# Left-overs of x ahead of the biases, row maxima sent from ScalarE's queue, ones around the first turn, Hadamard products two steps later

## The reference, cut to what matters

```python
x = x + attn_a(layernorm(x))   # 16 heads of 16: softmax(Q K^T / 4) V Wo^T, with biases
x = x + ffn(layernorm(x))      # fwht(silu(x W1^T) * (x W3^T)) W2^T, 1024 hidden
x = x + attn_b(layernorm(x))   # gated running memory, decay 0.95
x = x + ffn(layernorm(x))      # the same weights again
```

## Time and profile before

| | |
|---|---|
| runs | 582.75, 585.02, 587.06 us |
| profiled execution | 586.45 us, of which the span from first to last instruction is 584.7 us |
| TensorE busy | 564.5 us (97% of the span), 3274 instructions |
| VectorE busy | 380.5 us (65%) |
| ScalarE busy | 304.8 us (52%) |
| GpSimd busy | 179.1 us (31%) |
| mean granted clock of TensorE | 0.991 |
| chain that ended last | PE 82%, ACT 5%, POOL 4%, DVE 3%, SPq 2% |

### The profile page before, as it was taken

How to read it: one execution, slowest core, us unless ns; L and a number is a source line. 1 busy time by engine, 2 the same in 40 slices (tenths; PEclk the granted TensorE clock), 3 DMA queues, 4 the chain that set the end, 5 groups by cost and what they waited for, 6 DMA issues and landing times.

```text
span 584.7 us, 8896 instructions
## 1 busy us (share of the span) xinstructions
PE 564.5 (97%) x3274; PEld 389.8 (67%) x3274; DVE 380.5 (65%) x730; ACT 304.8 (52%) x559; POOL 179.1 (31%) x207
## 2 busy tenths in 40 slices
PE   7999999999999987999999999999999999999997
PEld 4553343344335433368988888898777888888887
DVE  6787898888888896745453544558887436344333
ACT  2657878867886886752334232344445233424221
POOL 4351456552545397820101010014333010101000
PEclk9988999999999999999999999999999999999999
DMA  5246530330034130020000000000000010010101
GB/s 153 63 124 231 158 118 2 111 109 3 20 113 132 55 127 3 3 72 2 1 0 1 1 1 2 1 0 1 1 1 1 0 37 1 0 37 2 36 1 37
DMA packets 17995, 25.74 MB, mean 44 GB/s; under 512 B 3048, under 2 KB 11240, under 8 KB 17568
## 3 DMA queue, kind: packets, MB, share of 16 engines
q1 hardware_dynamic: 16768, 24.11, 12.6%
q10 hardware_dynamic: 1184, 1.05, 0.6%
HBM read 10.89 MB, written 5.24 MB: 28 GB/s over the span
## 4 chain that ended last, share of the span: by engine, by line
PE 82%; ACT 5%; POOL 4%; DVE 3%; SPq 2%; issue 2%; DMA 1%; DVEq 0%; POOLq 0%; ACTq 0%
PE PS L369 79%; PE PS L380 2%; POOL xTl L1253 1%; ACT xf L774 1%; DVE PR L1222 1%; ACT PR L890 1%; ACT qf L788 1%; ACT xTh L774 1%; DVE XNs L1007 1%; ACT PR L953 1%; DMA ring<-mT 1%; POOL xf L1301 1%; DVE mxr L1026 1%; POOL XNs L1302 1%; SPq L258 1%
## 5 line engine op out<-in xcount | busy, mean ns | idle before, releaser
L369 PE MATMUL PS<-xTh,ring 128*128 128x512 f32 x608 | 188.7, 392 | 0.0
L1026 DVE TENSOR_REDUCE mxr<-PS 128x1 f32<-128x512 f32 x256 | 163.1, 681 | 30.7 <-PE PS L369 30.1
L890 ACT ACTIVATE PR<-PS 128x512 f32<-128x512 f32 x256 | 138.5, 602 | 41.6 <-PE PS L369 41.5
L369 PEld LDWEIGHTS PS<-xTh,ring 128*128 128x128 f32 x608 | 113.2, 188 | 23.6 <-issue 1.7
L369 PE MATMUL PS<-xTl,ring 128*128 128x512 f32 x304 | 110.3, 391 | 0.4 <-POOL xTl L1253 0.4
L369 PE MATMUL PS<-ring 48*128 48x512 f32 (+1 forms) x512 | 101.3, 456 | 6.2 <-DVE mxr L1026 4.4
L1171 DVE TENSOR_TENSOR PR<-PR,PS 128x512 f32<-128x512 f32 x64 | 43.8, 684 | 90.7 <-PE PS L369 71.0
L369 PEld LDWEIGHTS PS<-ring 50*128 50x128 f32 (+1 forms) x512 | 42.1, 187 | 85.1 <-ACT PR L890 57.2
L774 ACT ACTIVATE AOh<-PR 128x512 fp32r<-128x512 f32 x72 | 45.5, 632 | 101.8 <-DVE PR L1171 89.8
L1253 POOL TENSOR_TENSOR xTl<-xf,xTh 128x512 fp32r<-128x512 f32 x30 | 43.3, 1457 | 138.3 <-ACT xTh L774 138.3
L1018 DVE TENSOR_TENSOR AOl<-PR,AOh 128x512 fp32r<-128x512 f32 x72 | 51.1, 710 | 50.3 <-ACT AOh L774 50.3
(11 more groups left out here) (135 smaller groups left out, 629.8 us busy)
## 6 DMA issues: line engine op xcount, KB each, us to landing
ring<-qh SPq DMA_DIRECT2D x48, 128.0 KB, 2.7
ring<-ql SPq DMA_DIRECT2D x24, 128.0 KB, 2.7
ring<-weight_scratch SPq DMA_DIRECT2D x3, 1024.0 KB, 4.9
weight_scratch<-in_w SPq DMA_DIRECT2D x2, 1024.0 KB, 6.7
X<-in_x SPq DMA_DIRECT2D x3, 512.0 KB, 6.6
out<-X SPq DMA_DIRECT2D x6, 256.0 KB, 2.2
ring<-AOh SPq DMA_DIRECT2D x8, 128.0 KB, 2.7
ring<-AOl SPq DMA_DIRECT2D x4, 128.0 KB, 2.7
```

What stands on the lines that cost most here:

```text
L369: return nc.tensor.matmul(dst, lhsT, rhs, start=start, stop=stop, skip_group_check=True)
L890: nc.scalar.activation(PR[:, j % 8, :], PS[:, kq_bank(j), :], ACT.Exp, scale=HD ** -0.5)\
L1026: nc.vector.tensor_reduce(mxr[:, S % 2, blk, TT * p + t:TT * p + t + 1], PS[:, QK0 + i % 3, :], AX.X, ALU.max, negate=True).then_inc(max_d ...
```

## The change

Six edits.

- **VectorE, start:** the left-overs of x (`xTl`) are taken before the wait for the bias DMAs and `sbm`. Of the four statistics of sequence 1, two move behind `stack_rows(0)` and `(1)`.
- **TensorE, start:** stacks 0 and 1 first do the four products with `xTh` each, then the two with `xTl` each. TensorE waits for both halves of `x_hi` ahead of the first. In the other projections the order is the same as before. ScalarE does `stack_hi(1)` before it rounds the second weight matrix.
- **First maxima rows:** the pair of DMAs for `mrow_in` of the first group is issued by ScalarE, directly behind the copy into `mT`, and not by SyncE.
- **Ones:** at U = 10 and U = 12 of the lead, TensorE does one `keep_busy` of 384 columns.
- **Hadamard products:** `HAD_AT` goes from (14, 16, 26, 28) to (16, 17, 26, 28); ScalarE's copies and GpSimd's left-overs of the first two go with them (GpSimd's to steps 17 and 18, where the second stands behind the division of step 18). `output_lo(6)` goes from step 6 to step 13.
- **Weights:** the four left-overs of W3 (`W_LIN`) are taken by VectorE, each behind its own cast at steps 23 to 26, and GpSimd keeps the four of W1.

```diff
-HAD_AT = (14, 16, 26, 28)
+HAD_AT = (16, 17, 26, 28)
...
+            pe.wait_ge(x_hi, 2)
+            for i in range(2):
+                pe.wait_ge(swlo_done, i + 1)
+                project_stack(i, False)
+            pe.wait_ge(x_lo, 2)
+            for i in range(2):
+                project_stack(i, True)
...
+                else:
+                    keep_busy(1, PS[:, 0, :], FILL)
...
-            pe.wait_ge(llo_done, 8)
+            pe.wait_ge(llo_done, 4)
+            pe.wait_ge(lin_done, 4)
...
+            stack_hi(1)
             weights_hi(1)
-            stack_hi(1)
...
             max_evacuate(0, OB)
+            act.wait_ge(mt_ready, 1)
+            for blk in range(2):
+                act.dma_start(*max_copy(0, blk)).then_inc(mrow_in, DMA)
...
+            for dt in range(KD):
+                dve.wait_ge(x_hi, dt + 1)
+                lo(xTl[:, 0, dt, :], PS[:, dt, :], xTh[:, 0, dt, :]).then_inc(x_lo, 1)
             dve.wait_ge(mask_done, 1)
             dve.wait_ge(sbias_in, 8 * DMA)
...
-            for t in range(TT):
+            for t in range(2):
+                tile_statistics(TT + t, TT + t)
+            stack_rows(0)
+            stack_rows(1)
+            for t in range(2, TT):
                 last = tile_statistics(TT + t, TT + t)
...
                 nc.vector.tensor_copy(h, raw.bitcast(F32)).then_inc(lhi_done, 1)
+                if w == W_LIN:
+                    dve.wait_ge(lhi_done, 4 * w + i + 1)
+                    lo(raw, raw.bitcast(F32), h).then_inc(lin_done, 1)
...
-                if s == 6 and b:
+                if s == (13 if b == BATCH - 1 else 6) and b:
                     output_lo(2 * b)
...
-                if b == BATCH - 1 and SPLIT_AT <= s < SPLIT_AT + 8:
+                if b == BATCH - 1 and SPLIT_AT <= s < SPLIT_AT + 4:
```

More of the change, by code:

```diff
@@ L164, in build @@
         w_in = [sem(f"w_in{g}") for g in range(3)]
-        lhi_done, llo_done, mem_hi, mem_lo = (sem(n) for n in ("lhi_done", "llo_done", "mem_hi", "mem_lo"))
+        lhi_done, llo_done, lin_done, mem_hi, mem_lo = (
+            sem(n) for n in ("lhi_done", "llo_done", "lin_done", "mem_hi", "mem_lo"))
         g_ready, u_ready, sg_done, hf_done, hh_done, hl_done, y_ready = (
@@ L240, in rest_rows, with max_copy @@
                     for r in zip(*(rows(qk, part, blk) for blk in range(2))) for blk, r in enumerate(r)]
+        def max_copy(S, blk):
+            b, g = S // GROUPS, S % GROUPS
+            r = HALF * blk + MROW
+            return ring[r:r + 2, b % 2, QI, 2 * g:2 * g + 2, :].bitcast(F32), mT[16 * blk:16 * blk + 16, :]
         block = ctx.enter_context(nc.Block())
@@ L274, in _, with ring_load @@
                                  AOf[0:2, :].unsqueeze(1).broadcast_to([2, PAIRS - p, SEQ])).then_inc(ones_in, DMA)
-            def ring_load(b, n, parts_=range(2)):
-                for part in parts_:
+            def ring_load(b, n):
+                for part in range(2):
                     sp.wait_ge((qk_hi, qk_lo)[part], 4 * b + n + 1)
@@ L282, in max_rows @@
             def max_rows(S):
-                b, g = S // GROUPS, S % GROUPS
                 sp.wait_ge(mt_ready, S + 1)
                 for blk in range(2):
-                    r = HALF * blk + MROW
-                    sp.dma_start(ring[r:r + 2, b % 2, QI, 2 * g:2 * g + 2, :].bitcast(F32),
-                                 mT[16 * blk:16 * blk + 16, :]).then_inc(mrow_in, DMA)
+                    sp.dma_start(*max_copy(S, blk)).then_inc(mrow_in, DMA)
             def weights_in(w):
@@ L307, in _ @@
             ring_load(0, 2)
-            ring_load(0, 3, (0,))
-            max_rows(0)
-            ring_load(0, 3, (1,))
+            ring_load(0, 3)
             for e in range(2):
@@ L399, in project_qk, with project_rows, project_stack, project_rest @@
                     last.then_inc(qk_ready, 1)
-            def project_rows(weights, bank, first):
-                ops = [(1, 1, 0), (0, 1, 0), (1, 1, 1), (0, 1, 1), (0, 0, 0), (0, 0, 1)]
+            def project_rows(weights, bank, left):
+                ops = [(0, 0, 0), (0, 0, 1)] if left else [(1, 1, 0), (0, 1, 0), (1, 1, 1), (0, 1, 1)]
                 for i, (lo, r, kt) in enumerate(ops):
[L405 to L409, removed]
+                    last = mm(PS[:, bank, :], weights(lo, kt), xt(0, kt)[r], i == 0 and not left, i == 1 and left)
                 return last
-            def project_stack(i):
+            def project_stack(i, left):
                 p, w = i // 2, i % 2
-                project_rows(lambda lo, kt: stack_weights(lo, w)[:, kt, p * P:(p + 1) * P], STACK_BANK[i], i == 0)\
-                    .then_inc(stk_ready, 1)
+                last = project_rows(lambda lo, kt: stack_weights(lo, w)[:, kt, p * P:(p + 1) * P], STACK_BANK[i], left)
+                if left:
+                    last.then_inc(stk_ready, 1)
+            def project_rest(left):
+                last = project_rows(lambda lo, kt: rest_weights(lo)[:, kt, :], REST_BANK, left)
+                if left:
+                    last.then_inc(qk_ready, 2)
             def project_v(b, half, part, bank=MB):
@@ L508, in _ @@
             pe.wait_ge(pad_done, 1)
[L509 to L512, removed]
+            pe.wait_ge(x_hi, 2)
[5 more added lines that the diff above has]
+                project_stack(i, True)
             pe.wait_ge(rwlo_done, 1)
-            project_rows(lambda lo, kt: rest_weights(lo)[:, kt, :], REST_BANK, False).then_inc(qk_ready, 2)
+            for left in (False, True):
+                project_rest(left)
             def beside_maxima(U):
                 if U < 2:
-                    project_stack(2 + U)
+                    for left in (False, True):
+                        project_stack(2 + U, left)
                 elif U < 6:
@@ L1056, in _ @@
                                     ALU.mult).then_inc(sbm_done, 1)
-            for dt in range(KD):
-                dve.wait_ge(x_hi, dt + 1)
-                lo(xTl[:, 0, dt, :], PS[:, dt, :], xTh[:, 0, dt, :]).then_inc(x_lo, 1)
             def stack_rows(i):
```

4 lines of the change are left out of this document (1 added, 3 removed).

## The result

| | before | after |
|---|---|---|
| median of ten runs | 587.07 us (582.75 to 588.72) | 582.76 us (581.49 to 583.29) |
| profiled execution | 586.45, span 584.7 | 581.49, span 579.7 |
| mean granted clock of TensorE in it | 0.991 | 1.00 |

What follows compares the result with a forecast made beforehand. TensorE, busy nearly all the time, was taken as the bound, so gains come only where it waits or runs slowly. 586.45 - 3.05 - 0.15 - 3.3 - 1.6 + 2.7 = 581.0 us, range 578.5 to 584.4.

Steps and rivals of the forecast that it cites:

- Start, 3.05: Start: TensorE's wait for x's left-overs goes, first score at 15.3, 22 maxima from 21.0; 3.05 us gained, low clock included.
- Turn, 0.15: Turn: maxima's rows land earlier from ScalarE, ones fit beside the maxima's pace, TensorE arrives at 37.95; 0.15 us gained.
- Clock behind the turn, 3.3: Behind the turn: with the 1.03 us idle filled, clock stays at 1.00, steps 1 to 5 take 5.44; 3.3 us gained.
- First two products, 1.6: Last batch: the 2.61 us wait before the first Hadamard product goes, 0.5 before the second is new; net 1.6 us gained.
- Last two products, 2.7 lost: Last batch: left-overs on VectorE delay the third and fourth Hadamard products; 2.7 us lost, bound below 1.1.
- Rival 3: Last batch: new waits in steps 26 and 28 lower the clock, 3.4 us at half speed costing 1.7: 582.7; chance 0.12.
- Or the clock falls anywhere: Sign for the whole kernel: the prediction is wrong if TensorE's clock falls at any place; no size given.
- Rival 1: Behind the turn: the clock still falls, so the 3.3 us is not gained: 584.3; chance 0.17.
- rival 2: Last batch: VectorE has room for its left-overs, so the loss is only 1.1: 579.4; chance 0.14.
- Rival 4: Last batch: VectorE's left-overs held up like the worst casts, 1.15 each, 4.6 more: 585.6, slower than before; chance 0.07.

Runs made afterwards that it cites:

- late left-overs: Kernel after with VectorE's four left-overs of W3 moved behind its last reading of a Hadamard product: 579.40 us, ratio 0.987.
- the best of all: Kernel after with W3's left-overs behind VectorE's last Hadamard reading and ScalarE's two maxima-row DMAs behind its second copy of values: 578.92 us, ratio 0.9897.

## Why the prediction was right

- **What bounds the kernel.** Right: what was won and lost came from waits of TensorE, from the order of its start or from its clock, in the three places named, and arrived at the end (5.01 us at the fourth product, 5.0 in the span).
- **The sum.** 5.4 foretold, 5.0 measured in the profiles. In part this is luck: three gains were priced 0.06, 0.39 and 0.46 too high and the loss 0.55 too high, and more than half of the error cancels.
- **Start, 3.05.** Right to 0.06, and the marks with it (first score 15.37 for 15.3, the row of maxima 21.11 for 21.0). I put the gain down to the left-overs of x; the run with them moved back shows that the order of the stacks carries it in a good execution. The sum included the low clock behind the old wait, and rightly for the execution that I read: the run with the weights edit alone, where it did not fall, has its row of maxima at 22.71, so that 1.4 of the 2.99 are the clock and 1.6 the new order. In an execution like that one the start gains only 1.6.
- **Turn, 0.15.** Mis-sized: -0.24. I took 1.3 us for ScalarE's two DMAs from SyncE's row of 1.38; they took 1.92. The sentence "the transpose that waits for it then starts about where it does today" failed by that: the copy of values came at 32.84 and TensorE waited 0.63 for it.
- **Clock behind the turn, 3.3.** The mechanism is right and shown: with the ones 1.00, without them 0.50 for ten microseconds. The size is 2.84, since steps 1 to 5 took 5.95 (42.60 less 36.65) and not 5.44: the eight scores of steps 1 and 2 took 1.83, where eight take 1.33 later on, and I had taken the second batch's pace for theirs. Of these 0.5 us a wait of 0.15 for ScalarE, at 38.06, has a row; the rest stays open. What keeps the clock is the ones, not the earlier rows of maxima (without the ones it fell in eleven of twelve runs, with SyncE's rows and the ones it was 0.999 or 1.00 in five of six); for the rows the prediction named a gain in time of 1.6 us that nobody was waiting for once the start was earlier and the ones were in place.
- **First two products, 1.6.** Right in the execution profiled (1.57, with the wait of 0.51 for the 0.5 foretold).
- **Last two products, 2.7 lost.** Right in sign, in place and in who waits for whom; the size is 2.15. The waits are 0.57 and 1.48, where I had 0.9 and 1.6. Counted from the output projection of step 18, the add came 1.63 late (11.47 against 9.84) where I had 1.9. The first two left-overs took 2.35 and not 1.5, and a cast at 227.93 took 1.40 beside GpSimd's second product's left-over; against that, GpSimd was through at 235.54, so that the sixth cast took 0.41 and only one left-over of VectorE stood beside its three. The last two took 0.69 and 0.98.
- **Rival 3** was underrated with 0.12: by the mean clock something like it happened in half of the runs, and the median, 582.76, is its 582.7 and not the forecast's 581.0. "Or the clock falls anywhere" was moreover among the signs named for being wrong. "Against: the 2.61 before the first product did not" was read from one execution. That wait lowered the clock in four of the five profiles that have it (the start, the turn and the weights edit alone, and the late left-overs with the old Hadamard steps; not in before) and, by the mean clock, in eleven of twelve runs of the last of these. That the lower half of the clocks of the kernel after belongs to the new waits is inferred: from the second window without the ones, and from the twelve runs of the two kernels that lack these waits, none of which was below 0.999. The kernel before moved too, from the median of three, 585.02, to 587.07 of ten. Both moved up, and so the difference stayed near the forecast, which is luck: 5.4 foretold, 4.3 on the medians, 3.8 by the ratio.
- **Rivals 1, 2 and 4** did not happen. Rival 1 does as soon as the ones are taken out; rival 2's time of 579.4 is reached, by another way than its own, when the left-overs are placed behind the readings. Rival 4's price of 1.15 a left-over was met by the first alone (1.66 less 0.69 is 0.97).

## What to carry to other kernels

Put work that an engine takes over behind the last instruction that somebody waits for, not beside the instruction that feeds it: the same four left-overs cost 2 us in one place and nothing in the other. Price a wait of the matrix engine twice, once for its length in every run, and once for the clock behind it in a part of the runs, and look at several runs' mean clock before saying that a wait leaves the clock alone. Price a gain that includes a low clock as two numbers, since an execution in which the clock does not fall pays only the smaller one. When one edit makes the start earlier, ask of each edit behind it whether the thing that it speeds up is still late.

## What the runs showed of the hardware

- **The clock falls in some executions and not in others of the same kernel.** It fell behind a wait of 1.77 us (and not behind 1.78 in another kernel's profile), behind 1.03, behind 0.81 and 0.42, behind 0.57 and 1.47 (and not behind 0.57 and 1.48), and behind 2.58 to 2.61 (and not behind 2.61 in before). Once it fell at 22.8 us, with no wait in TensorE's rows for the 7 us ahead of it. The stretches at 1.2 GHz were 3.4 to 27 us long. Three kernels whose profiles have no wait over 0.65 us behind the first 8 us (all left-overs on GpSimd, late left-overs, and the best of all) stayed at 0.999 or 1.00 in all of six runs each, with spreads of 0.4, 0.3 and 1.1 us, where the kernel before spreads over 11.0 us (580.70 to 591.69 in 35 runs). Others of that kind did not quite: one of six runs was at 0.979 (591.79 us), one of six at 0.997 (580.44), two of eleven at 0.997. So a longer wait makes a fall likely here, and its absence does not rule one out.
- **VectorE's left-overs wait for GpSimd like its casts.** 0.69 us alone, 1.66 beside GpSimd's row of three. The Trainium skill, "SBUF — State Buffer", section "Who interferes with whom", says that the port pair that the two engines share is an exclusive lock; the rows agree, and for the smallest operation too. `sbm`, four columns wide, took 0.85 in the earlier trace rows; in the kernel after it took 0.51 and ended with GpSimd's left-over; in the run with the late left-overs and the old order at the start it ended just as that one began, and took 0.16. VectorE and GpSimd of the kernel after:

```profile
11.81 0.51 DVE L1074 TENSOR_TENSOR sbm<-sbias,smask 128x4 f32<-128x4 f32 x1
```

```profile
10.99 1.31 POOL L1274 TENSOR_TENSOR WAl<-qf,WAh 128x512 fp32r<-128x512 f32 x1 [0.34 <-ACT WAh L787]
```

- **Issuing this pair of DMAs costs ScalarE more than SyncE:** 0.96 us each (1.92 for the pair, 1.86 to 2.11 in nine profiles) against 0.69 (1.38 in the earlier trace rows, and 1.38 again with the rows through SyncE), and ScalarE's next activation stands behind it.
